# Two recurrences of a twelve-layer kernel: the memory scan rewritten with two chunks per transfer, and every third product of the selective scan moved to GpSimd

## The reference, cut to what matters

```
# L1_attn: selective scan, 512 channels x 16 states
dA = exp(dt_t[:, :, None] * A)
h  = dA * h + (dt_t[:, :, None] * B_t[:, None, :]) * z_t[:, :, None]
y_t = einsum('bds,bs->bd', h, C_t)

# L2_attn: memory scan, 16 heads of 16 x 16
upd = (1.0 - k)[..., :, None] * v[..., None, :]
kv  = scan over t of  kv = k * kv + upd
h   = einsum('nthd,nthde->nthe', q, kv)
```

## Time and profile before

| | |
|---|---|
| median of three runs | 5646.16 us (5633.03 to 5648.47) |
| the profiled execution's own time | 5625.59 us |
| its span, first to last instruction | 5623.8 us |
| mean granted TensorE clock | 0.914 |
| busy over the span | PE 4835.9, DVE 3154.1, ACT 2112.5, POOL 916.4 us |

### The profile page before, as it was taken

One profiled execution on the slowest core, in us unless ns is written; L12 is line 12 of the kernel. 1 busy time (PEld: TensorE's weight loads), 2 busy tenths in 40 slices (PEclk: granted clock), 3 DMA queues, 4 the chain that ended last, 5 costly groups with the idle time before them and its releaser, 6 DMA issues. The chain is left out here.

```text
span 5623.8 us, 114522 instructions
## 1 busy us (share of the span) xinstructions
PE 4835.9 (86%) x45678; PEld 3696.2 (66%) x45678; DVE 3154.1 (56%) x5754; ACT 2112.5 (38%) x4043; POOL 916.4 (16%) x487
## 2 busy tenths in 40 slices
PE   6879999998669989999765999986579989998877
PEld 4659888895559956666312788875159956665365
DVE  5358777772544455555397433454953456665453
ACT  1235555551135534445232333342024434444121
POOL 0023222220002200000064222141612200000200
PEclk8889999999679999999899999998669999999986
DMA  1010000000111021110122111033311110000120
GB/s 59 29 35 15 19 18 15 22 1 27 49 38 52 30 54 38 49 38 26 36 71 57 45 52 45 22 81 67 97 43 45 37 31 26 26 26 33 30 69 30
DMA packets 197892, 222.92 MB, mean 40 GB/s; under 512 B 45299, under 2 KB 166980, under 8 KB 189284
## 3 DMA queue, kind: packets, MB, share of 16 engines
q1 hardware_dynamic: 193380, 208.54, 12.2%
q10 hardware_dynamic: 4096, 8.40, 0.6%
HBM read 170.09 MB, written 15.34 MB: 33 GB/s over the span
## 5 line engine op out<-in xcount | busy, mean ns | idle before, releaser
L2367 DVE TENSOR_REDUCE block_max<-PS 128x1 f32<-128x512 f32 (+1 forms) x896 | 505.2, 626 | 300.7 <-PE PS L2227 300.4
L2316 ACT ACTIVATE probs_turned<-PS 128x512 f32<-128x512 f32 (+1 forms) x896 | 434.5, 571 | 563.4 <-PE PS L2248 563.3
L1632 PE MATMUL PS<-input_part,part_up 128*128 128x512 f32 x2304 | 552.4, 392 | 18.4 <-DVEq L1713 8.6
L1645 PEld LDWEIGHTS PS<-part_down,hidden_part 128*128 128x128 f32 x4608 | 548.6, 188 | 2.1
L1645 PE MATMUL PS<-part_down,hidden_part 128*128 128x256 f32 x4608 | 549.1, 281 | 0.0
L1685 ACT ACTIVATE hidden<-PS,b 128x512 f32<-128x512 f32 x384 | 264.5, 689 | 652.7 <-PE PS L1632 637.2
L1632 PEld LDWEIGHTS PS<-input_part,part_up 128*128 128x128 f32 x2304 | 434.7, 189 | 110.5 <-DVEq L1713 9.3
L844 PE MATMUL PS<-context_turned,queries 128*128 128x512 f32 x1728 | 411.0, 382 | 23.9 <-issue 17.2
L876 PE MATMUL PS<-probs_turned,context_part 128*128 128x256 f32 (+2 forms) x3120 | 409.2, 286 | 3.7 <-DVE weighted L953 3.7
L1721 DVE TENSOR_TENSOR hidden_part<-hidden,hidden_part 128x512 fp32r<-128x512 f32 x384 | 293.6, 774 | 182.9 <-ACT hidden_part L1675 182.2
L905 ACT CAST probs_turned<-PS 128x512 fp32r<-128x512 f32 x576 | 261.3, 510 | 356.7 <-PE PS L856 356.7
(11 more groups left out here) (422 smaller groups left out, 8113.7 us busy)
## 6 DMA issues: line engine op xcount, KB each, us to landing
context_rows<-in_ctx SPq DMA_DIRECT2D x40, 768.0 KB
raw_up<-in_L_ffn_W SPq DMA_DIRECT2D x16, 1024.0 KB, 4.8
raw_down<-in_L_ffn_W SPq DMA_DIRECT2D x16, 1024.0 KB, 4.8
ctx_turned<-context_turned SPq DMA_DIRECT2D x16, 800.5 KB, 4.7
context_turned<-ctx_turned SPq DMA_DIRECT2D x16, 800.5 KB
b_all<-bc_turned SPq DMA_DIRECT2D x32, 256.0 KB, 3.5
c_all<-bc_turned SPq DMA_DIRECT2D x32, 256.0 KB, 4.3
raw_up<-in_L_ffn_wg_w SPq DMA_DIRECT2D x8, 1024.0 KB, 4.8
```

The source lines that it names most:

```text
L1632: last = nc.tensor.matmul(PS[:, k % ring + 2 * x, :], bank.parts[name][a][:, c, f * P:(f + 1) * P], h[b][:, c, half * 512:(half + 1) * 512 ...
L1645: last = nc.tensor.matmul(PS[:, 4 + t % outs, 0:DIM], aT[a][:, f, t * P:(t + 1) * P], bank.parts["down"][b][:, f, :], start=(f == 0 and m ...
L2316: nc.scalar.activation(probs[0:kk, t % ring, i, 0:many].rearrange("p k c s -> p (k c s)"), PS[0:kk, bank_of("turned", t, i), 0:many * 2 * ...
L2367: nc.vector.tensor_reduce(part[:, b % 2, chunks[0]:chunks[-1] + 1, i, u // 2], bank, AX_X, ALU.max).then_inc(max_done.sem, 1)
```

## The change

In the selective scan `fresh` is made for two chunks in one GpSimd instruction (2 x 512 elements, ring of three pairs), and of the items n with n % 3 = 1 the state goes to SBUF (`state_held`, ring of two) and GpSimd makes the product with C; the ring `prod` grows from 3 to 8.

The memory scan is rewritten for D_t = S_t - v_(t+1), which follows D_t = k_t D_(t-1) + (v_t - v_(t+1)): the difference is taken once, in a block of its own between the linears of v and q (`dropT`), and the product with 1-k goes. What the shift leaves out is put back by a correction out of v, sums of q over a head, and the cumulated product of k (`cumulated`, `q_sums`, `cumulated_sums`). k is copied to PSUM once (`keep`) and the DVE scans from there; the products with q are on GpSimd. All DMAs are issued by SP, one per head and e for both chunks (16 partitions x 2 x 4 KB), into a ring of four.

```diff
@@ -2572,12 +2572,12 @@
-    ring, rows_ring = 3, 4
+    ring, pairs, prod_ring, held_ring, rows_ring = 3, 3, 8, 2, 4
...
-    state_bank = lambda n: PS[:, C + 2 + n % 2, :]
+    by_pool = lambda n: n % 3 == 1
+    before = lambda n, pool: sum(by_pool(k) == pool for k in range(n))
+    state_at = lambda n: held[:, n // 3 % held_ring, :] if by_pool(n) else PS[:, C + 2 + before(n, False) % 2, :]
+    def taken(n):
+        return (g_ready.sem, g_ready.at(before(n, True) + 1)) if by_pool(n) else (w_ready.sem, w_ready.at(before(n, False) + 1))
...
-        fresh = core.sb(own, "fresh", [P, ring, wide])
-        prod = core.sb(own, "prod", [P, ring, wide])
+        fresh = core.sb(own, "fresh", [P, pairs, 2, wide])
+        prod = core.sb(own, "prod", [P, prod_ring, wide])
+        held = core.sb(own, "state_held", [P, held_ring, wide])
...
-                        sp.wait_ge(w_ready.sem, w_ready.at((r - rows_ring + 1) * C))
+                        last = (r - rows_ring + 1) * C
+                        sp.wait_ge(w_ready.sem, w_ready.at(before(last, False)))
+                        sp.wait_ge(g_ready.sem, g_ready.at(before(last, True)))
...
-                for n, (h, s, c) in enumerate(items):
+                def product(n):
+                    h, s, c = items[n]
+                    pool.wait_ge(h_ready.sem, h_ready.at(n + 1))
+                    if n >= prod_ring:
+                        pool.wait_ge(summed.sem, summed.at(n - prod_ring + 1))
+                    nc.gpsimd.tensor_tensor(prod[:, n % prod_ring, :], state_at(n), Cb[:, n // C % rows_ring, :],
+                                            ALU.mult).then_inc(g_ready.sem, 1)
+                for n in range(0, len(items), 2):
+                    h, s, c = items[n]
                     r = n // C
                     if c == 0:
                         pool.wait_ge(landed[r % rows_ring].sem, landed[r % rows_ring].at(32 * (r // rows_ring + 1)))
-                    if n >= ring:
-
-                        pool.wait_ge(h_ready.sem, h_ready.at(n - ring + 1))
-                    nc.gpsimd.tensor_tensor(fresh[:, n % ring, :], dtz[:, c, cols(h)], Bb[:, r % rows_ring, :],
+                    if n >= 2 * pairs:
+                        pool.wait_ge(h_ready.sem, h_ready.at(n - 2 * pairs + 2))
+                    nc.gpsimd.tensor_tensor(fresh[:, n // 2 % pairs], dtz[:, c:c + 2, cols(h)],
+                                            Bb[:, r % rows_ring, :].unsqueeze(1).broadcast_to([P, 2, wide]),
                                             ALU.mult).then_inc(in_ready.sem, 1)
+                    for k in (n - 4, n - 3):
+                        if k >= 0 and by_pool(k):
+                            product(k)
+                for k in range(len(items) - 4, len(items)):
+                    if by_pool(k):
+                        product(k)
...
-                    dve.wait_ge(in_ready.sem, in_ready.at(n + 1))
-                    nc.vector.tensor_tensor_scan(state_bank(n), decay_bank(n), fresh[:, n % ring, :], 0.0,
+                    dve.wait_ge(in_ready.sem, in_ready.at(n // 2 + 1))
+                    if by_pool(n) and n >= 3 * held_ring:
+                        dve.wait_ge(*taken(n - 3 * held_ring))
+                    nc.vector.tensor_tensor_scan(state_at(n), decay_bank(n), fresh[:, n // 2 % pairs, n % 2, :], 0.0,
...
-                    product(n)
+                    if not by_pool(n):
+                        product(n)
...
+        normalize(core, X, U, loads=w.loads, clear=firstT, turned=(uT, None, None))
         linear_turned(core, uT, w["L2_attn_v_w"], vT)
+        vector_steps(core, [
+            lambda: v.tensor_tensor(by_batch(dropT)[:, :, 0:SEQ - 1], by_batch(vT)[:, :, 0:SEQ - 1],
+                                    by_batch(vT)[:, :, 1:SEQ], ALU.subtract),
+            lambda: v.tensor_copy(by_batch(dropT)[:, :, SEQ - 1:SEQ], by_batch(vT)[:, :, SEQ - 1:SEQ])])
         linear_turned(core, uT, w["L2_attn_q_w"], qT,
-                      stores=[(core.dram["v_turned"].rearrange("(c p) n -> p c n", p=P), vT[:])])
+                      stores=[(core.dram["v_turned"].rearrange("(c p) n -> p c n", p=P), dropT[:])])
         linear_turned(core, uT, w["L2_attn_key_w"], kT, w["L2_attn_key_b"], ACT.Sigmoid)
         vector_steps(core, [
-            lambda: v.tensor_scalar(freshT[:], kT[:], -1.0, 1.0, ALU.mult, ALU.add),
-
-            lambda: v.memset(kT[:].rearrange("p c (b s) -> p c b s", s=SEQ)[:, :, :, 0:1], 0.0)])
-        memory_scan(core, kT, freshT, qT, w["gather_rows"], uT, d)
+            lambda: v.tensor_copy(by_batch(firstT)[:, :, 0:1], by_batch(kT)[:, :, 0:1]),
+            lambda: v.memset(by_batch(kT)[:, :, 0:1], 0.0)])
...
+    ring, prod_ring, rows_ring = 3, 6, 4
...
+    keep = lambda c: flat(PS[:, fills + c * HALVES:fills + (c + 1) * HALVES, :])
...
+                for e in range(d):
+                    u = e % rows_ring
+                    if e >= rows_ring:
+                        sp.wait_ge(h_ready.sem, h_ready.at((e - rows_ring + 1) * DC))
+                    for h in range(per):
+                        sp.dma_start(Vb[h * d:(h + 1) * d, :, u, :],
+                                     vrows[h, e:e + 1].broadcast_to([d, DC, TOKENS])).then_inc(landed[u].sem, 16)
...
+                for c in range(DC):
+                    nc.scalar.copy(keep(c), kT[:, c, :]).then_inc(k_moved.sem, 1)
+                for n, to in enumerate((q_sum, cum_sum)):
+                    for f in range(fills):
+                        act.wait_ge(sums_ready.sem, sums_ready.at(n * fills + f + 1))
+                        nc.scalar.copy(to[:, f // HALVES, f % HALVES * 512:(f % HALVES + 1) * 512],
+                                       PS[:, f, :]).then_inc(sums_taken.sem, 1)
...
+                wait_weights(core, pool)
+                nc.gpsimd.tensor_tensor(pairs[:], gather[:, 0:8, :], gather[:, 8:16, :], ALU.add).then_inc(head_sums_ready.sem, 1)
+                for k, many in enumerate((4, 2, 1)):
+                    pool.wait_ge(head_sums_ready.sem, head_sums_ready.at(k + 1))
+                    nc.gpsimd.tensor_tensor(pairs[:, 0:many, :], pairs[:, 0:many, :], pairs[:, many:2 * many, :],
+                                            ALU.add).then_inc(head_sums_ready.sem, 1)
+                pool.wait_ge(cum_ready.sem, cum_ready.at(DC))
+                for c in range(DC):
+                    nc.gpsimd.tensor_tensor(cum[:, c, :], cum[:, c, :], qT[:, c, :], ALU.mult).then_inc(cum_product.sem, 1)
+                for n, (e, c) in enumerate(items):
+                    pool.wait_ge(h_ready.sem, h_ready.at(n + 1))
+                    if n >= prod_ring:
+                        pool.wait_ge(summed.sem, summed.at(n - prod_ring + 1))
+                    nc.gpsimd.tensor_tensor(prod[:, n % prod_ring, :], state[:, n % ring, :], qT[:, c, :],
+                                            ALU.mult).then_inc(w_ready.sem, 1)
...
+                for c in range(DC):
+                    dve.wait_ge(k_moved.sem, k_moved.at(c + 1))
+                    nc.vector.tensor_tensor_scan(cum[:, c, :], keep(c), firstT[:, c, :], 0.0, ALU.mult,
+                                                 ALU.add).then_inc(cum_ready.sem, 1)
+                def correction():
+                    dve.wait_ge(sums_taken.sem, sums_taken.at(2 * fills))
+                    nc.vector.tensor_tensor(by_batch(q_sum)[:, :, 0:SEQ - 1], by_batch(q_sum)[:, :, 0:SEQ - 1],
+                                            by_batch(vT)[:, :, 1:SEQ], ALU.mult).then_inc(step.sem, 1)
+                    nc.vector.memset(by_batch(q_sum)[:, :, SEQ - 1:SEQ], 0.0).then_inc(step.sem, 1)
+                    nc.vector.tensor_tensor(by_batch(cum_sum), by_batch(cum_sum),
+                                            by_batch(vT)[:, :, 0:1].broadcast_to([P, DC * BATCH, SEQ]),
+                                            ALU.mult).then_inc(step.sem, 1)
+                    dve.wait_ge(step.sem, step.at(3))
+                    nc.vector.tensor_tensor(q_sum[:], q_sum[:], cum_sum[:], ALU.subtract).then_inc(step.sem, 1)
+                for n, (e, c) in enumerate(items):
+                    u = e % rows_ring
+                    if n == 2 * DC:
+                        correction()
+                    dve.wait_ge(landed[u].sem, landed[u].at(16 * per * (e // rows_ring + 1)))
+                    if n >= ring:
+                        dve.wait_ge(w_ready.sem, w_ready.at(n - ring + 1))
+                    nc.vector.tensor_tensor_scan(state[:, n % ring, :], keep(c), Vb[:, c, u, :], 0.0,
+                                                 ALU.mult, ALU.add).then_inc(h_ready.sem, 1)
+                dve.wait_ge(summed.sem, summed.at(len(items)))
+                dve.wait_ge(step.sem, step.at(4))
+                nc.vector.tensor_tensor(dst[:].rearrange("p c n -> p (c n)"), flat(PS[:, 0:fills, :]),
+                                        q_sum[:].rearrange("p c n -> p (c n)"), ALU.add).then_inc(step.sem, 1)
...
```

(52 more changed lines are left out.)

90 lines of the change are left out of this document (18 added, 72 removed).

## The result

The changed kernel takes 5561.84 us in the median of four runs (5550.32 to 5576.56), against 5640.19 for the kernel before on the same chip: a ratio of 0.9862 [0.9833, 0.9891], 78 us less. Its profiled execution took 5562.66 us, with a span of 5560.9 and a mean granted clock of 0.912 (before: 5625.59, 5623.8 and 0.914).

A forecast was written before the change was run, and what follows sets the result against it. It took the VectorE to pace the selective scan, and exclusion between GpSimd and VectorE instructions with two SBUF inputs the memory scan. -28 - 52.5 + 4 = -76.5 us from 5646.2 gave 5570 us, range 5538 to 5602.

The forecast's parts named there:

- The selective scan, -28: Selective scan: 43 products moved to GpSimd save the VectorE 29.7 us, less 1.1 at the start and 0.6 at the end.
- the cover is thin: Selective scan: GpSimd would need 204 us against the VectorE's 209, with an upper end of 212.
- The memory scan, -52.5: Memory scan: without exclusion, transfers bound it at 133 GB/s, 7.9 us a column; 142.3 us in total against 194.8.
- Ahead of it, +4: Before the memory scan: difference block +3, half clock at q's linear +2, product 1-k gone -1.1.
- the rate is 133 and not 166: Memory scan's transfers: one queue writing two chunks to the same 16 partitions moves 133 GB/s, not 166; 7.9 us a column.
- The first rival: Memory scan's transfers: two queues slow by taking turns, so one keeps 166 GB/s; 25 us less, 5544; chance 0.20.
- Faster transfers: Memory scan: a single queue keeps 166 GB/s or more; 6.3 us a column, 25 us less, 5544; chance 0.20.
- the slower ones of 109 GB/s: Memory scan: each 64 KB always costs 0.60 us; 27 us more, 5597; chance 0.11.
- the slow single queue: Memory scan: one queue carries only half of 133 GB/s, by a limit of its own; +126 us, 5696; chance 0.04.
- The exclusion: Both scans: a scan reading PSUM and writing SBUF might still exclude GpSimd; +41 and +21 us, 5632; chance 0.05.

The follow-up runs named there:

- every second product: The changed kernel with every second product of the selective scan on GpSimd, 64 instead of 43: 5572.99 us, 0.9890.
- the run without refills: The changed kernel fetching only the memory scan's first four columns and reading them again for the twelve later ones: 5503.67 us in one run.
- two queues apart: The changed kernel with 64 KB DMAs, chunk 0 from SP, chunk 1 from ScalarE's queue beginning four heads further on: 5534.45 us, 0.9793.
- the in-step run: The changed kernel with 64 KB DMAs, one chunk from SP and one from ScalarE's queue, both beginning at the same head: 5545.46 us in one run.
- the order in pairs: The changed kernel with its heads' DMAs in the order 0 2 1 3 4 6 5 7, neighbours 32 partitions apart: 5586.61 us in one run.

## Why the prediction was right

**The total.** Forecast 5570, measured 5561.84, and a ratio that puts the change at -78 us for -76.5. That is closer than the working deserves, and in part luck. Against the first profile the memory scan gained 9.0 us more than its term, the selective scan 2.3 less, and the part ahead lost 4.8 more. These misses cancel to 2 us, and part of that is the clock in a layer that no edit touched. The ratio's interval alone allows any gain from 61 to 94 us, so the total confirms no single term; the stages do that. Of the 8.2 us between 5570 and 5561.84, 6.0 come from the median of before, which was 5646.16 in the forecast and is 5640.19 here.

**The selective scan, -28.** From the first scan to the last gate product it lost 26.8 us, and the first scan waits 1.1 longer for its input, as forecast: 25.7 in all. That lies between the bounds of -31 and -24, the first of which has no working. The product that went saved 0.74 us of the VectorE's time and not the 0.69 of its own length (31.8 us in all), but from a scan to its product 1.31 us pass now in the mean, 1.27 before; over 85 products that gives back 3 us. The end cost 1.3 where I had put 0.6. The layer gained 24.5, a little less: the first scan begins 100.8 us into it for 99.6, and the linear behind the scan took 16.81 us for 15.74 in the same 64 records. GpSimd's load was 203.9 us for the forecast 204, its double input 2350 ns for 2.34 us. That the cover is thin is shown by every second product: it made GpSimd the bound.

**The memory scan, -52.5.** This is the term that was mis-sized most: 142.3 us forecast, 133.3 measured (4032.81 less 3899.48), so -61.5 us for -52.5. The first column landed after 9.8 us and not 10.7; the fifteen others took 112.1 and not 118.5 (7.5 us each, not 7.9, the rate rising from 136 to 148 GB/s); and the tail took 11.4 and not 13.1, since TensorE's last four records ran in 1.98 us and not in 3.8. The mechanism was right in each point: scans of 2.28 us, no exclusion, the VectorE idle 3.2 us per column behind the DMA, everything else hidden. The forecast that free transfers would leave 82 us for the loop's 118.5 has its test in the run without refills, 30.4 us less, against some 30 by that sum from the measured 112.1.

**Ahead of it, +4.** From the layer's start to SP's first issue 38.5 us passed before and 40.6 after: +2.1. The block cost 2.8 us of TensorE's idling and the slow start of q 2.6. But the v linear took 7.11 us, not 9.03, at a higher clock. In the second profile the v linear took 8.54 and q's 8.80, and SP's first issue came 41.6 us after the layer's start, +3.2. What no term had is the layer ahead, 6.7 us longer in the first profile and 2.5 in the second: with it this part is 8.8 in the one and 5.7 in the other, for the +4 of the forecast. The prediction's clause that the v difference might move the clock of more than q's linear doesn't cover that layer, which lies ahead of the difference.

**Why the rate is 133 and not 166.** The step from the earlier trace rows, that DMAs which write the same partitions one after the other are slow, fits every run here. That it is the two chunks within one DMA that slow the single queue was not tested by itself. The first rival's reason, that two queues slow each other by taking turns, is refuted: two queues apart ran at 167 to 205 GB/s. That the slow rate holds for two queues in step and for one queue alike is shown by the in-step run. What I had not seen was that heads 32 partitions apart, two heads on, also share something, which the order in pairs showed.

**The rivals.** Faster transfers and the slower ones of 109 GB/s did not come; nor did the slow single queue. The exclusion is real, but a PSUM input lifts it for a scan too, whether it writes PSUM or SBUF (1214 ns for both beside GpSimd in the selective scan, 2277 in the memory scan).

**Where span and median part.** The two profiled spans differ by 62.9 us and the medians by 78. The profile of before was a quick one (the second one of it was 13.8 us longer, 11.3 of them ahead of the selective scan's layer), and that of after had the three slow layers. The two scans' layers alone give -24.5 - 59.3 = -83.8. The second profile of the changed kernel gives -71.4 against the first of before, -85.2 against the second.

## What to carry to other kernels

When transfers bound a stage, look at which partitions the DMAs in flight write before counting queues or bytes: here the same 16.8 MB passed at 120 or 137 GB/s on one queue, and at 134 to 140 in step or 167 to 205 apart on two, with nothing but the order changed within each pair. An operand moved to PSUM can take the VectorE and GpSimd out of each other's way, but then ask at once what comes next, and let the trace's own stretches with a backlog price it. And compare stages, not spans: a clock that steps in layers which no edit touched can hide 26 us.

## What the runs showed of the hardware

- Two queues that broadcast rows to 16 partitions at a time move 167 to 205 GB/s when they are four heads apart, 134 to 140 when they keep to the same head; one queue with 128 KB for each head 136 to 148, and with neighbours 32 partitions apart 120; one queue alone with 64 KB for each head 165, for 6 us.
- With two SBUF inputs a 1024-element scan beside a busy GpSimd takes 4011 ns in the mean; with one of them in PSUM 2277. Of two VectorE instructions in turn it can be either that is held up: 4300 and 1286 ns in one execution, 2346 and 3225 in another.
- TensorE's granted clock in an untouched layer differs between two executions of one program: the same linear in 15.3 or 9.0 us.
